# Padding the row vectors and their 12-row matmul operand with zero rows to 128 rows, in a two-layer graph network with residual and layer norm on one core

## What is computed

```python
def _mp_layer(x, src, dst, edge_attr, W, b):
    n = x.shape[0]
    loops = jnp.arange(n, dtype=src.dtype)
    src2 = jnp.concatenate([src, loops])
    dst2 = jnp.concatenate([dst, loops])
    ea2 = jnp.concatenate([edge_attr, jnp.zeros((n, edge_attr.shape[1]), dtype=edge_attr.dtype)], axis=0)
    x_i = x[dst2]
    x_j = x[src2]
    msg = jnp.concatenate([x_i, x_j, ea2], axis=1) @ W + b
    agg = jax.ops.segment_sum(msg, dst2, num_segments=n)
    return jax.nn.relu(agg)
src, dst = (edge_index[0], edge_index[1])
h = _mp_layer(x, src, dst, edge_attr, W1, b1)
h = jax.nn.relu(h)
out = _mp_layer(h, src, dst, edge_attr, W2, b2)
return jax.nn.log_softmax(out, axis=1)
```

## Time and profile before

| | |
|---|---|
| median of 3 runs | 209.03 us (208.85 to 209.24) |
| the profiled execution | 208.97 us, its span 207.2 us |
| busy PE, PEld | 177.4 us (86%), 162.7 us (79%) |
| busy DVE | 173.8 us (84%) |
| busy ACT, POOL | 118.8 us (57%), 48.9 us (24%) |
| mean granted clock of TensorE | 0.994 of full speed |

### The profile page before, as it was taken

How to read it: one execution, slowest core, us unless ns; L and a number is a source line. 1 busy time by engine, 2 the same in 40 slices (tenths; PEclk the granted TensorE clock), 3 DMA queues, 4 the chain that set the end, 5 groups by cost and what they waited for, 6 DMA issues and landing times.

```text
span 207.2 us, 5086 instructions
## 1 busy us (share of the span) xinstructions
PE 177.4 (86%) x2019; PEld 162.7 (79%) x2019; DVE 173.8 (84%) x495; ACT 118.8 (57%) x234; POOL 48.9 (24%) x56
## 2 busy tenths in 40 slices
PE   0515399999999999999899999999996999999950
PEld 0104299888988989889779889798996999999940
DVE  0889999999999999999999989921019999999873
ACT  2336649778997997888889989984220201111101
POOL 8388998305000692003004000000000000000000
PEclk9999999999999999999999999999999999999997
DMA  1334101000000000000000000000000010011010
GB/s 41 106 93 116 24 4 36 0 4 2 3 0 4 0 5 0 3 1 3 0 4 0 5 0 3 2 3 0 3 0 0 3 30 10 3 40 25 22 22 20
DMA packets 8886, 3.32 MB, mean 16 GB/s; under 512 B 8146, under 2 KB 8411, under 8 KB 8861
## 3 DMA queue, kind: packets, MB, share of 16 engines
q1 hardware_dynamic: 8061, 2.04, 4.8%
q0 software_dynamic: 800, 0.93, 1.9%
HBM read 2.15 MB, written 0.81 MB: 14 GB/s over the span
## 4 chain that ended last, share of the span: by engine, by line
PE 61%; DVE 29%; issue 3%; ACT 3%; DMA 2%; DVEq 0%; ACTq 0%
PE pset L1016 17%; PE acc L975 15%; PE pset L961 13%; DVE ohr L514 8%; DVE ohl L514 7%; PE acc L1016 7%; PE epb L1002 3%; PE epb L1010 2%; DMA adj<-in_dst 2%; PE epb L990 2%; DVE adj L504 2%; ACT adj L816 1%; DVE adj L463 1%; PE epb L1003 1%; PE epb L992 1%
## 5 line engine op out<-in xcount | busy, mean ns | idle before, releaser
L816 ACT ACTIVATE adj<-pset 125x1000 bf16<-125x1000 f32 (+7 forms) x100 | 81.1, 836 | 15.1 <-PE pset L961 12.0
L975 PE MATMUL acc<-x,adj 125*125 125x195 bf16 x625 | 67.8, 252 | 0.0
L961 PE MATMUL pset<-ohr,ohl 128*125 128x125 bf16 x625 | 54.4, 232 | 8.7 <-DVE ohr L514 8.1
L961 PEld LDWEIGHTS pset<-ohr,ohl 128*125 128x125 bf16 x625 | 47.7, 146 | 13.8 <-issue 6.6
L975 PEld LDWEIGHTS acc<-x,adj 125*125 125x125 bf16 x625 | 57.1, 139 | 0.3
L514 DVE TENSOR_TENSOR ohl<-iota,keys 128x1000 bf16<-128x1000 bf16 (+1 forms) x79 | 52.5, 664 | 0.7 <-ACT keys L799 0.5
L514 DVE TENSOR_TENSOR ohr<-iota,keys 128x1000 bf16<-128x1000 bf16 (+1 forms) x79 | 52.5, 664 | 0.0
L1016 PE MATMUL pset<-z,adj 125*125 125x192 bf16 x425 | 37.0, 247 | 1.8 <-DVE x L661 1.8
L1016 PEld LDWEIGHTS pset<-z,adj 125*125 125x125 bf16 x425 | 35.5, 136 | 2.4 <-DVE x L661 2.0
L903 ACT ACTIVATE x<-x 125x192 f32<-125x192 f32 (+2 forms) x6 | 2.6, 427 | 34.5 <-DVE x L670 34.5
L384 POOL CAST stats<-se 125x15 bf16<-125x15 f32 x5 | 5.4, 1071 | 54.3 <-DMA se<-se_scratch 54.3
(11 more groups left out here) (120 smaller groups left out, 169.3 us busy)
## 6 DMA issues: line engine op xcount, KB each, us to landing
x_nat<-in_x_tiles SPq DMA_DIRECT2D x1, 406.2 KB
x_nat<-in_x_tiles SPq DMA_DIRECT2D x1, 375.0 KB
out<-x SPq DMA_DIRECT2D x2, 187.5 KB
out<-x SPq DMA_DIRECT2D x3, 93.8 KB
adj<-in_dst SPq DMA_DIRECT2D x1, 208.5 KB
out<-x SPq DMA_DIRECT2D x1, 125.0 KB
adj<-in_edges,adj POOLq DMA_INDIRECT x5, 4.3
adj<-in_edge_attr,adj POOLq DMA_INDIRECT x5, 3.5
```

Source lines behind the costliest of these rows:

```text
L816: ins = act.activation(adj4[0:Q, g, :, i * WD:(i + n) * WD].rearrange("p h (w e) -> p h w e", e=WD), rows[:, w - k * SET:w - k * SET + n, ...
L961: ins = pe.matmul(pset[k % 2][0:Q, i // 4, i % 4 * 128:i % 4 * 128 + WD * G], ohl[k % 3][:, i // 2, :, i % 2], ohr[k % 3][:, i // 2, :, i ...
L975: ins = pe.matmul(acc[g % 2][0:Q, 0:XW], adj4[0:Q, g, h, :], x3[:, h, :], start=(h == 0), stop=(h == G - 1))
```

## The change

`vt` and `bw` are allocated with 128 rows in place of 12. POOL fills both with zeros, ahead of the three fills of `x3`, and counts `zeros_ready`. DVE writes the same 12 rows of `bw` as before, and ACT the same 12 rows of `vt`; DVE before the first of its writes, and ACT before its first copy, wait for the zeros too. The matmul of L1003 is written as before, and now has 128 rows in both operands. The rows that are added are zeros, and so add nothing to the result.

```diff
-        bw = sb("bw", [KB, HID], BF16)
+        bw = sb("bw", [128, HID], BF16)
...
-        vt = sb("vt", [KB, EP * Q], BF16)
+        vt = sb("vt", [128, EP * Q], BF16)
...
+        zeros_ready = sem("zeros_ready")
...
                     [[Q * WD, J], [1, WD], [0, 2]], base=0, channel_multiplier=WD).then_inc(loops_ready, 1)
+            gp.memset(vt[:, :], 0.0).then_inc(zeros_ready, 1)
+            gp.memset(bw[:, :], 0.0).then_inc(zeros_ready, 1)
             gp.memset(x3[:, :, C:XC], 1.0).then_inc(consts, 1)
...
                     dve.wait_ge(bp_ready, 3)
+                    dve.wait_ge(zeros_ready, 2)
                     dve.wait_ge(bmask_ready, 1)
...
-                    dve.scalar_tensor_tensor(out=bw[:, :], in0=bpart[:, 2, :], scalar=bmask[:, 2:3], in1=r1,
+                    dve.scalar_tensor_tensor(out=bw[0:KB, :], in0=bpart[:, 2, :], scalar=bmask[:, 2:3], in1=r1,
...
                 act.wait_ge(t_ready, i + 1)
+                if i == 0:
+                    act.wait_ge(zeros_ready, 2)
                 act.activation(flat(i)[:, 0:n], epb[:, 0, 0:n], ACT.Copy)
-                act.activation(vt[:, 0:n], epb[0:KB, 1, 0:n], ACT.Copy).then_inc(ut_ready, 1)
+                act.activation(vt[0:KB, 0:n], epb[0:KB, 1, 0:n], ACT.Copy).then_inc(ut_ready, 1)
```

## The result

| | before | changed |
|---|---|---|
| median | 209.03 us | 207.38 us (206.96 to 207.68, 4 runs) |
| the profiled execution, its span | 208.97 us, 207.2 us | 207.35 us, 205.5 us |

The ratio is 0.9919, with a 95% interval of 0.9899 to 0.9939: faster, by 1.65 us. The forecast was 207.2 us. The page of the changed kernel has

The account below looks back on a forecast made before the run. PE (86% busy) and DVE (84%) were both nearly full. Savings of 1.87 us less 0.05 us for the opening gave 1.82 us, taking 208.97 to 207.15 us; the median's 0.06 us made 207.2 us, range 206.5 to 208.2 us.

Parts of the forecast that it names:

- The gap: PE around each of L1003's nine matmuls: idle time on both sides goes, saving 0.24 us each, bounds 0.22 and 0.26 us.
- The rival that only part goes: Around L1003: only some idle time or savings count, 1.2 us (207.8 us) or 0.96 us (208.0 us); chance 0.18.
- the one that nothing goes: Around L1003: the gap has a cause other than the 12 rows and stays, 209.0 us; chance 0.11.
- What reaches the end: Whole kernel, followed through waits between PE and DVE: of 2.16 us saved on PE, 1.87 us shortens the run.
- the cap by DVE's waits: Before 101 us: PE is 0.72 us early after three L1003 matmuls, but DVE can use only 0.67 us.
- place 4: Fourth L1003 matmul, 91.9 us: its saving only makes PE wait longer for DVE at 101.07 us, so worth nothing.
- Places 6 to 9: Last four L1003 matmuls, from 118.25 us through the transition to layer 2: all count, together 0.96 us.
- The opening: First microseconds: POOL's idle 3.02 us before the first gather covers its two fills; loss 0.05 us, bounds 0 and 0.94.
- The slower rival: Gap stays and POOL's two fills delay DVE (4.7 to 5.7 us) or the gather: up to 209.9 us; chance 0.05.
- The bounds of the forecast: Total time: own range 206.8 to 207.6 us; full range 206.5 (all nine matmuls in full) to 208.2 us.
- No idle time before the next load: Sign of being right, on the weight loader: no idle time before L1003's load nor before the load behind it.
- One of the signs of being wrong: In the opening: the first set coming later than before would show the forecast wrong.

## Why the prediction was right, and where not

- **The gap, and what removes it: shown.** It goes on both sides, 0.25 us a place in the chain (0.24 was forecast), and by the rows alone. The rival that only part goes, and the one that nothing goes, are out.
- **What reaches the end: 2.04 us, not 1.87.** From set 17 (0.36 us late) to the seventh group (1.68 us early) the profile gained 2.04 us; the same kernel with 12 rows gained nothing there (0.36 us late, then 0.37). Up to set 44 it was 0.64 us, forecast 0.67: the cap by DVE's waits held. The step that failed is place 4, "worth nothing". It was worth 0.2 us, since a wait of DVE too short for the idle list stood there; PE's wait at the set of 101 us grew by 0.08 us (0.74 to 0.82), not by the whole 0.24. Places 6 to 9 gave 0.97 us, forecast 0.96.
- **The opening: 0.50 us, not 0.05.** This is the term that was mis-sized, by a factor of ten. I looked for POOL's delay on POOL, where idle time did cover it, and took the bound of 0.94 us for DVE's delay as unlikely, with no row for it. The conversion itself, 0.57 us long beside three small fills, was already held up, and I compared it with nothing. The slower rival's mechanism (fills that delay DVE) is thus real; at 0.5 us it could have decided only if the gaps had stayed, as the runs with 12 to 64 rows show.
- **The sum.** 2.04 - 0.50 = 1.54 us; the profile shows 1.68, since between sets 4 and 17 the changed kernel won 0.13 us, by PE's speed-up as told below. Two errors, +0.17 and -0.45, partly cancelled, and the speed-up was in no forecast; that 207.2 us lies only 0.18 us from the median is in part luck. The bounds of the forecast were also added up loosely: 0.26 us a place and a free opening give 0.69 + 0.26 + 1.04 = 1.99 us, which is 207.0 us and not 206.8, and nine times 0.26 us is 206.7 us, not 206.5 or 206.6.
- **The signs.** "No idle time before the next load" was wrong as a sign: 0.22 us stands there and costs nothing. One of the signs of being wrong did appear: PE's first sets came later than before, at 17.25 us instead of 16.75. That is the opening's 0.50 us, and the forecast held in spite of it.

## What to carry to other kernels

In this kernel a short matmul of 12 to 64 rows, or of 12 weight columns, between full-height ones cost about 0.25 us beside its own time, and zeros or unread neighbours that filled it up took that away. Look for it in the chain of waits, in what the same matmuls take behind it and behind another. Keep POOL's fills away from DVE's critical conversions, by another engine or another moment, and judge them by DVE's durations rather than by POOL's idle time.

## Not expected

- POOL's fills hold DVE's conversion up until they are done: 1.16, 0.57 and 0.39 us for the same instruction beside five, three and no fills. The Trainium skill, "GPSIMD Engine Reference", Key points, says that POOL shares its SBUF interfaces with DVE and contends with DVE instructions in a 2-port mode or with two inputs. The runs agree in that the conversion, which has one tensor input, was held up; whether it ran in such a mode no run shows. The one-hots, with two inputs, were not slowed by two of the same fills (0.67 us), and no run here explains that.
- PE speeds up at a moment of its own. The timeline of PE, kernel before:

```profile
27.95 1.06 PE L961 MATMUL pset<-ohr,ohl 128*125 128x125 bf16 x8
...
31.51 0.64 PE L961 MATMUL pset<-ohr,ohl 128*125 128x125 bf16 x8
```

The granted clock reads 1.00 (the level of 2.4 GHz) in all windows from 16 to 34 us, so it doesn't show this. PE had been working in short bursts, with 1.0 to 2.3 us of idle time between them, until some 26 us, and without a break from then on. The first quick set began at 29.36 us with POOL's fills early, at 30.20 in the changed kernel, 31.51 in the one before, 32.01 with ACT's fills. At set 11, and with what each had at set 4 taken off, the profiles stand 0.15 us ahead of the kernel before, level with it, or 0.2 us behind it, whatever their edit. The profile with the small fills moved is one of those behind and the one without the move is one of those ahead, which is where its 0.20 us of the opening went. That the medians differ for this reason is likely and not shown; what fixes the moment stays open, and no run varied it on purpose.
